# Two transformer layers on one core: the first attention's turned probabilities regrouped by rows, seven products with the values, and a new order of all tasks

## The reference, cut to what matters

```python
sim = jnp.einsum('bhid,bhjd->bhij', q, k) + rel * slopes
sim = jnp.where(causal, mask_value, sim)
attn = jax.nn.softmax(sim, axis=-1)
out = jnp.einsum('bhij,bhjd->bhid', attn, v)
```

## Time and profile before

| what | value |
|---|---|
| time, median of 3 runs | 2472.6 us (2466.52 to 2473.21) |
| the profiled execution's own time | 2475.11 us |
| its span, first to last instruction | 2473.2 us |
| granted TensorE clock, mean | 0.982 |
| PE busy | 2349.1 us, 32,896 matmuls |
| DVE, ACT, POOL busy | 1832.7, 1876.5, 1443.5 us |

### The profile page before, as it was taken

One profiled execution on the slowest core, in us unless ns is written; L12 is line 12 of the kernel. 1 busy time (PEld: TensorE's weight loads), 2 busy tenths in 40 slices (PEclk: granted clock), 3 DMA queues, 4 the chain that ended last, 5 costly groups with the idle time before them and its releaser, 6 DMA issues.

```text
span 2473.2 us, 82166 instructions
## 1 busy us (share of the span) xinstructions
PE 2349.1 (95%) x32896; PEld 1136.1 (46%) x32896; DVE 1832.7 (74%) x5637; ACT 1876.5 (76%) x4707; POOL 1443.5 (58%) x1356
## 2 busy tenths in 40 slices
PE   6999999999999999999999999999999999999877
PEld 3554444444544444444444544444444444544322
DVE  5568687787877778687787877778786887877674
ACT  4877877877778787877878777887777877787434
POOL 5975574756648466574756657475574756556201
PEclk9999999999999999999999999999999999999877
DMA  3011020200202020020201102020020201102020
GB/s 100 4 38 23 7 58 3 57 6 20 45 3 62 3 57 8 6 58 3 62 3 29 36 7 57 3 57 7 7 58 3 62 2 40 25 3 57 2 56 5
DMA packets 59946, 70.45 MB, mean 28 GB/s; under 512 B 11056, under 2 KB 55344, under 8 KB 56368
## 3 DMA queue, kind: packets, MB, share of 16 engines
q1 hardware_dynamic: 59568, 65.21, 11.4%
HBM read 35.04 MB, written 29.36 MB: 26 GB/s over the span
## 4 chain that ended last, share of the span: by engine, by line
PE 77%; DVE 16%; ACT 3%; issue 2%; DMA 1%; SPq 0%; POOL 0%; POOLq 0%; DVEq 0%; ACTq 0%
PE pj L1595 18%; PE pj L1691 12%; PE sc L1659 10%; PE pj L1721 10%; PE sc L1676 5%; PE sc L1768 5%; PE pj L1707 5%; DVE mx L1362 5%; PE pj L1615 5%; PE sc L1754 4%; DVE pq L1309 4%; PE pj L1585 3%; ACT pt L1044 1%; DVE y L1330 1%; DVE onrm L1372 1%
## 5 line engine op out<-in xcount | busy, mean ns | idle before, releaser
L845 POOL TENSOR_SCALAR pq<-pq,rsum 128x128 f32<-128x128 f32 (+3 forms) x1024 | 1151.8, 1139 | 772.8 <-DVE rsum L1316 771.2
L1362 DVE TENSOR_REDUCE mx<-sc 128x1 f32<-128x512 f32 x1024 | 644.1, 679 | 247.5 <-PE sc L1768 247.1
L996 ACT ACTIVATE pq<-pq,mx 128x128 f32<-128x128 f32 (+3 forms) x1024 | 569.8, 570 | 25.9 <-DVE mx L1309 25.7
L1044 ACT ACTIVATE pt<-sc 128x512 f32<-128x512 f32 x1024 | 543.9, 607 | 36.0 <-PE sc L1754 34.6
L1309 DVE CUSTOM_DVE_ANT_0 pq<-sc,relkey 128x128 f32<-128x128 f32 (+3 forms) x1024 | 448.5, 484 | 158.7 <-PE sc L1659 156.1
L1014 ACT ACTIVATE pt<-sc 128x512 f32<-128x512 f32 (+1 forms) x768 | 376.6, 535 | 162.3 <-PE sc L1676 159.5
L1659 PE MATMUL sc<-K,Q 64*128 64x128 f32 (+3 forms) x2048 | 362.5, 452 | 15.7 <-DVE mx L1309 9.4
L1691 PE MATMUL pj<-pt,v 128*32 128x512 f32 (+3 forms) x4096 | 303.8, 437 | 8.5 <-DVE y L1330 5.7
L1676 PEld LDWEIGHTS sc<-ident,pq 64*128 64x128 f32 x5120 | 200.1, 138 | 189.8 <-issue 99.7
L1595 PE MATMUL pj<-xnT,wqkv 128*32 128x512 f32 x2048 | 263.1, 606 | 4.0 <-ACT xnT L947 2.0
L1676 PE MATMUL sc<-ident,pq 64*128 64x64 f32 x5120 | 234.6, 227 | 7.4 <-DVE mx L1309 4.0
(11 more groups left out here) (117 smaller groups left out, 2836.7 us busy)
## 6 DMA issues: line engine op xcount, KB each, us to landing
scr_p<-y SPq DMA_DIRECT2D x160, 128.0 KB, 2.4
QS<-scr_p SPq DMA_DIRECT2D x30, 384.0 KB, 5.8
KS<-scr_p SPq DMA_DIRECT2D x30, 384.0 KB, 8.5
x_in<-in_L_attn_x SPq DMA_DIRECT2D x16, 256.0 KB, 2.9
scr_p<-tanh SPq DMA_DIRECT2D x32, 128.0 KB, 2.4
out_x<-xres SPq DMA_DIRECT2D x15, 256.0 KB, 2.3
QS<-nrow SPq DMA_DIRECT2D x180, 4.0 KB
wqkv<-in_L_attn_w_qkv SPq DMA_DIRECT2D x1, 1536.0 KB, 6.5
```

Source lines behind the costliest of these rows:

```text
L845: pool.tensor_scalar(rows, rows, rsum[:, row_slot(i, p), c:c + 1], None, ALU.mult).then_inc(s_scl, 1)
L996: act.activation(rows, rows, ACT.Exp, scale=-1.0, bias=mx0[:, row_slot(i, p), c:c + 1], accum_out=lsum[:, row_slot(i, p), c:c + 1]).then_i ...
L1044: act.activation(pt1[:, 2 * (unit % UNITS) + h, :], sc[tile_bank(i, "st1", 2 * n + h)][:, :], ACT.Exp, scale=float(DS) ** -0.25).then_inc( ...
L1362: dve.reduce_max(mx1[:, g % 2, at:at + 1], sc[tile_bank(i, "mx1", 2 * t + h)][:, :], AXIS.X).then_inc(s_mxd1, 1)
```

## The change

Five things are changed together.

1. The groups of turned blocks go by row blocks: group 0 has key block 0 of rows 0, 1, 2; group 1 the other blocks of rows 1 and 2; group 2 all four blocks of row 3. With two heads that is 6, 6 and 8 blocks.
2. Groups 0 and 1 need six scalings (rows 0 to 2); only group 2 needs all eight.
3. `pv0` makes seven products where it made four: for rows 0 to 2 of width 384, 256 and 128, and for row 3 four of width 128.
4. On every engine the order of the tasks within a tick is another, with the orders in which the banks are handed out.
5. Nearly all tick constants are others, and the clocks part otherwise at the end.

```diff
-TURNED = (((0, 0), (1, 0)), ((0, 1), (0, 3), (1, 1), (1, 3)), ((0, 2), (1, 2)))
+TURNED = (((0, 0), (0, 1), (0, 2)), ((1, 1), (1, 2), (2, 2)), ((0, 3), (1, 3), (2, 3), (3, 3)))
+TURN_NEEDS = (6, 6, 8)
+PIECES = ((0, 0, 3), (1, 1, 3), (2, 2, 3), (0, 3, 4), (1, 3, 4), (2, 3, 4), (3, 3, 4))
...
-X_AT = -14
-LN0_AT = (-14, -9, -3)
+X_AT = -25
+LN0_AT = (-20, -8, -3)
-HT0_AT = -1
-FFN0_AT = (1, 2, 6, 7)
+HT0_AT = 1
+FFN0_AT = (2, 4, 6, 7)
...
-CLOCKS = (TICKS * NB + 7, (5, 4, 2), (2, 4, 0), (3, 5, 0), (11, 0, 11), (1, 8, 4))
+CLOCKS = (TICKS * NB + 6, (5, 3, 2), (2, 6, 0), (3, 5, 0), (9, 0, 11), (1, 17, 4))
...
             def turn_probs(i, p, g):
-                if g == 0:
-                    pe.wait_ge(s_scl, i.upto(L0N, 8 * p + 8))
+                if g != 1:
+                    pe.wait_ge(s_scl, i.upto(L0N, 8 * p + TURN_NEEDS[g]))
...
             def pv0(i, p):
-                for k in range(NT):
+                for k, q, past in PIECES:
...
-                            last = pe.matmul(t[r, P * k:T], v0[:, p % NBUF, k, r], pt[:, base:base + WIDTH[k]],
-                                             start=k == 0, stop=k == NT - 1)
+                            last = pe.matmul(t[r, P * q:P * past], v0[:, p % NBUF, k, r], pt[:, base:base + P * (past - q)],
+                                             start=k == 0, stop=k == past - 1)
```

More of the change, by code:

```diff
@@ L331, in pj_order @@
         elif late(g) and r == 2:
+            second(h, k, 0)
+            second(h, k, 1)
+            values(h, k, 0)
+            misc(g, h, k)
+            values(h, k, 1)
+            pairs("v", g, -1)
+        elif late(g) and r == 3:
+            values(h, k, 0)
+            second(h, k, 0)
+            second(h, k, 1)
+            values(h, k, 1)
+            misc(g, h, k)
+        elif r == 0:
+            pairs("q", g, -1)
+            pairs("k", g, -1)
+            second(h, k, 0)
+            values(h, k, 0)
+            second(h, k, 1)
+            misc(g, h, k)
+            values(h, k, 1)
+        elif r == 1:
+            second(h, k, 0)
+            second(h, k, 1)
+            pairs("pv", g, 3)
+            values(h, k, 0)
+            misc(g, h, k)
+            values(h, k, 1)
+        elif r == 2:
+            second(h, k, 0)
+            second(h, k, 1)
+            values(h, k, 0)
+            pairs("v", g, -1)
+            values(h, k, 1)
+            misc(g, h, k)
+        else:
             values(h, k, 0)
@@ L407, in score_order @@
         if late(g) and r == 0:
-            second_keys(h, k, 0)
+            turned(g, 2, 1)
+            second_tops(h, k, 0)
             tops(g, 0, 0)
[L410 to L416, removed]
             second_keys(h, k, 0)
@@ L419, in score_order @@
             second_keys(h, k, 1)
+        elif late(g) and r == 1:
+            second_tops(h, k, 0)
+            second_keys(h, k, 0)
+            turned(g, 2, 2)
+            second_keys(h, k, 1)
+            second_tops(h, k, 1)
         elif late(g) and r == 2:
@@ L1123, in tick @@
                         copy_attention(i, p)
+                    p, i = pair(g, 2)
+                    if i is not None:
+                        copy_turned(i, p, 5)
+                elif late(g) and r == 2:
+                    second_attention(h, k, 0)
                     p, i = pair(g, 0)
@@ L1831, in tick @@
                 if late(g) and r == 0:
-                    second_keys(h, k, 0)
+                    p, i = pair(g, 2)
+                    if i is not None:
+                        turn_probs(i, p, 1)
+                    second_tops(h, k, 0)
                     p, i = pair(g, 0)
@@ L1881, in tick @@
                         project_v(i, p)
+                elif late(g) and r == 3:
+                    p, i = pair(g, 1)
+                    if i is not None:
+                        turn_probs(i, p, 0)
                     p, i = pair(g, 0)
```

401 lines of the change are left out of this document (177 added, 224 removed).

## The result

The kernel after takes 2459.6 us (median of 9 runs, 2457.8 to 2463.0) beside 2474.1 us for the kernel before: a ratio of 0.9937, with a 95% interval of 0.9923 to 0.9951. That is 14 us faster, and 12.6 us above the 2447 predicted: inside the range, on the side forecast. Where the gain comes from is another matter.

What follows compares the result with a forecast made beforehand. PE, busy 95% of the span, was taken to bound the kernel. Per item -0.8 (kinds), -1.4 (banks), +0.4 (pieces) make -1.8; over 14 items -25 us, so 2447 us, range 2427 to 2464 (8 in 10: 2406 to 2488).

Steps and rivals of the forecast that it cites:

- The kinds: PE's changes between wide and halved work, 102 before and 88 after per item: -1.0 us per item, counted as -0.8.
- the pieces: Seven products for four in `pv0`, 24 more matmuls and loads per pair: +0.05 us per pair, +0.4 per item.
- the signs named: Item 145.6 us; `pv0` 2.15 to 2.35; queries plus keys 1.86; turned groups wait less for DVE; PE's POOL waits near zero.
- The rival of the pieces' loads: In `pv0`, the added weight loads show on PE: 79 us, giving 2520; chance 0.04.
- the banks: PE's waits for score banks that DVE or ACT must empty: -1.4 us per item, bounds -5 to +4.
- 14 are short, by 5.8 us: Of an item's 112 score-bank uses, 14 come back too early after the change, where 15 were short by 7.2 us.
- The first two items ... I leave at +0.4: Items with little or no second attention: left at +0.4 us, outside the 14 items given the full gain.
- the freed wait "at nothing": Turned groups 0 and 1 no longer wait for POOL's scaling of row 3: costed between -1.2 us and 0.
- regrouping alone would be ... at most 5 us slower: Rival: regrouping alone gives +6 - 1, at most 5 us slower; all the gain hangs on the order; no chance given.
- The end: Last stretch of the span, bound by latencies, same tasks in a new order: 0 +- 8 us.
- the 25 us forecast for the fourteen items: Items 2 to 15, where everything runs together: 14 x -1.8 us per item.

Runs made afterwards that it cites:

- the dose of ten products: `pv0` cut into ten products of 128 columns: in the kernel before, 2498.8 us (ratio 1.0099); in the kernel after, 2468.1 us (0.9966).
- experiment 9: Kernel after with row 2's exponentials moved on ACT from the end of r = 2 to behind r = 3's first second keys: 2512.2 us, ratio 1.0144.
- experiment 7: Kernel before with the first item's feed-forward tasks in the ticks of the kernel after: 2470.8 us, ratio 0.9975.
- experiments 1: Kernel before with new groups, weaker wait and seven products: 2486.1 us; kernel after with old groups, old wait and four products: 2585.9 us.
- experiment 3: Kernel before with only the seven products; old groups, wait and order: 2486.3 us, ratio 1.0046.
- experiment 2: Kernel after with all eight scalings awaited again ahead of the first two turned groups: 2572.0 us, ratio 1.0385.
- seven with wide values: Kernel before with seven products and the second layer's values projected in one piece of 512 columns instead of four of 128: 2482.1 us, ratio 1.0030.

## Why the prediction was right, and where it was not

**Right: PE's own work.** The kinds and the pieces were to change PE's own time by -1.0 and +0.4 us per item (the sum counts 0.8 of the 1.0); PE without waits fell by 0.65, 9 us over 14 items. Task by task the shortest distances agree: query projections give some 0.6 us per item and the second scores 1.2, while the first scores take back 0.4, as forecast, and `pv0` 0.3. This is read from the two traces; no run changes the kinds alone. Four of the signs named came: 1.86 us for queries and keys, 2.30 for `pv0`, no wait of PE for POOL in the trace after (it lists none), and turned groups that wait less for DVE's emptying (PE's idle there 5.3 us before, 1.0 after). The fifth, 145.6 us for an item, did not: 146.8. The rival of the pieces' loads (79 us) fell: 24 more matmuls and loads cost 0.01 to 0.02 us per pair where nothing stops PE, below the 0.05 taken. The 60 cycles per matmul of the Trainium skill (TensorEngine Tiling (Array Packing), Instruction Overhead) would be 0.6 us per pair, as an estimate from that page; the dose of ten products speaks against it once more.

**Wrong: the banks.** The step "14 are short, by 5.8 us ... so -1.4 us per item" failed: waits are 10.8 us before and after. The largest wait went as forecast, but new ones came in ticks 15 and 16 and others, behind ACT's second exponentials (94.8 to 141.4 us over the span). I compared PE's time to the third use of a bank with the emptying instruction alone; what else stands in ACT's queue between two emptyings was left out, and a task more in ACT's queue in r = 3 makes the kernel slower, as experiment 9 shows.

**Wrong: the start.** "The first two items ... I leave at +0.4". They gave -7.4, of which experiment 7 shows 5.9 as the place of the first item's feed-forward tasks. The earlier trace rows had no stretch of the start; the wait of 5.5 us for weights was in the trace, and the constants that move it are in the diff. That the time came out nearer than its working is luck: of the 25 us forecast for the fourteen items 7 came, and 10 of the span's 17 stand at the start and the end, where the sum had none.

**Half right: the freed wait "at nothing".** For the old order that holds (experiments 1 and 3). For the new one it is worth 112 us (experiment 2), because that order lets the scalings come later. The prediction said that its worth is indirect and gave it no price; the rival "regrouping alone would be ... at most 5 us slower" was short too (10 to 13).

**Missed: what seven products do to the old order.** It lost 10 to 12 us, in good part by stops of PE in ticks 25 and 26 (experiment 3), and the kernel before had some of them already: without a stop the two ticks take 8.09 us there, 113.3 in 14 items, and they took 116.9. After, they take 118.7, 1.0 more than 14 times the 8.41 of an item without a stop. This part of the order's worth was in no step.

**The end** (0 +- 8) was -2.7; but the profiles with the new order have 187.6 to 190.7 us there, those with the old one 189.9 to 193.2, so that one pair of profiles says little. No run tests it by itself.

**The clock** takes a little back. Stretch of the kernel after in item 2, before and during a fall:
```profile
288.00:289.20 1.20, 0.69 (x2) 0.18 (x2) 1.17 (x5) 1.20 (x4) 1.20 (x1) 1.00 0.00 0
289.20:292.40 3.20, 3.20 (x17) 0.52 (x16) 1.52 (x11) 3.20 (x8) 3.20 (x4) 0.57 0.03 6
```
Behind the new waits of ticks 15 and 16 the granted clock was 0.57 once, and the tick 1.4 us longer; a second fall stands in tick 10 of item 14, 1.2 us. The kernel before has none in these items.

What stays open: that the new order stops less because it sends the stacks' transfers apart is read from the traces (last section), and no run moves those transfers alone. No run changes the kinds on PE alone either.

## What to carry to other kernels

Price a weaker wait in the order that will use it: alone it was worth nothing, and the new order without it lost 112 us. When the banks of an engine are counted, count all that stands in that engine's queue between two emptyings, and read the first and last items as regimes of their own. Before a product is cut into more matmuls, look whether it stands in a dense stretch beside large transfers: there 24 matmuls cost 0.4 to 1.3 us per item (5.7 / 14 and 17.9 / 14, from the table), elsewhere 0.01 to 0.02 per pair.

## What the runs showed of the hardware that was not expected

PE can run out of instructions in the middle of a task. In items 2 to 15 of five kernels (before, seven products, ten products, seven with wide values, and the kernel after with ten), two successive matmuls of one group start more than 1 us apart, without a wait, in 18 places, all in tick 25. In each, PE goes on 1.23 to 1.48 us after a 16 KB packet of the instruction queue ended. The kernel after has no such place. The page's rows of that queue (packets, MB, share), for the kernel before and the one with ten products:
```profile
q8 instruction: 262, 4.29, 0.7%
```
```profile
q8 instruction: 310, 5.08, 0.9%
```
48 matmuls and 48 loads more per pair, 12,288 instructions, are 48 packets more in all: one packet for 256 instructions of PE. Instructions stream in all through the run, and a share under 1% of the DMA engines says nothing about how late one packet is.

The traces also show which instruction is late. If PE's instructions (matmuls, loads and waits) are counted in their order, all 18 stops stand at the 194th or 195th of a run of 256. Mostly the packet for the next such border starts about 0.3 us after PE passed the last one (the median in the kernel before). In the 18 cases it starts 4 to 9 us after, while the transfers of the stacks run out: their last data ends 0 to 1.1 us after its start. Two stretches of the run with seven products alone, from one border to the start of the packet and from there to where PE goes on (as above; last two columns: share of the DMA engines, GB/s):
```profile
777.15:784.12 6.97, 6.90 (x94) 3.51 (x96) 6.76 (x33) 6.53 (x16) 3.98 (x4) 1.00 0.97 159
784.12:787.00 2.88, 1.26 (x38) 0.98 (x30) 1.54 (x5) 1.22 (x6) 2.88 (x3) 1.00 0.02 3
```
So a stop takes three things together: a late packet, which comes with the transfers; a stretch dense in matmuls, in which PE uses up 256 instructions before it lands; and a border that falls into that stretch. Where the borders fall follows from the number of instructions: with seven products and wide values an item has 4544 of them, 17.75 packets, so a border comes back to the same place in every fourth item, and those are the items that stop. The old order issues the four stack transfers within some 3 us; the new one issues the last two some 9 us after the first two, and then they land sooner. The page's rows for those last two, before and after (KB each, us to landing):
```profile
KS<-scr_p SPq DMA_DIRECT2D x30, 384.0 KB, 8.5
```
```profile
KS<-scr_p SPq DMA_DIRECT2D x30, 384.0 KB, 5.7
```
In items 2 to 15, seven packets of the kernel before start over 4 us after PE passed the border before them, and one of the kernel after.
